# Attention in a five-stage convolution kernel: the receptance moved from a sigmoid and a gate into the column denominators

## The chip, the cores and the metric

The kernel runs on one core of a Trainium2 chip. Its engines are PE (matrix multiply), DVE (VectorE), ACT (ScalarE, which evaluates functions from a table that has to be loaded), POOL (GpSimd) and SP, which issues DMAs here. Each engine runs its own queue in order and waits on semaphores. The metric is the device time of one execution in microseconds, as the median of three runs.

## The reference

Two layers: a pointwise and a 13x13 depthwise convolution with GELU, then a block with attention and a feed-forward part, on 16 images of 192 channels and 56 x 56 pixels. What matters here is the attention:

```
k = xs2 @ att_wk.T
v = xs2 @ att_wv.T
sr = jax.nn.sigmoid(xs2 @ att_wr.T)
v = _wkv(sp_decay[0] / T, sp_first[0] / T, k, v)        # along rows
k2, v2 = k, v with rows and columns exchanged
v2 = _wkv(sp_decay[1] / T, sp_first[1] / T, k2, v2)     # along columns
v = v2 with rows and columns exchanged back
att_out = sr * v @ att_wo.T
tok = tok + gamma1 * att_out
```

`_wkv` is a recurrence over the 3136 pixels, channel by channel: a weighted running sum of v (numerator) over a running sum of weights (denominator), with a running maximum of the exponents to keep them in range. The last product is sr times the quotient of the column pass. With sr = 1 / (1 + exp(-r)), sr * N / D equals N / (D * (1 + exp(-r))).

## The kernel before

`build` runs six stages: `prepare`, `pointwise`, `depthwise` and `omni`, `attention`, a second `omni`, and `feed_forward`. Only `attention` (L820) is touched. It lies in the middle of the span.

**Tiles and steps.** The channels of two images make three tiles of 128 partitions; `TILES` is 24. A step s (0 to 24) does the row pass of tile s and the column pass of tile s-1. Each pass has 7 units of 448 pixels, so that a full step has 14 units, at positions 0 to 13; `ROWS_AT` = 3, 5, 6, 8, 9, 11, 12 are those by row, and 0, 1, 2, 4, 7, 10, 13 those by column. Step 0 has only rows, step 24 only columns.

**A unit.** DVE makes the running maximum O (`run_max`, a copy at L1259 or a memset at L1253, then the scan L1260), two units ahead. POOL subtracts it (`exponents`, L1203 and L1206). ACT exponentiates: L1109 gives the input factor E, L1114 the decay factor A. POOL multiplies E by v (`weigh`, L1216, into EV). DVE scans the sums Q and P (`sums`, L1265, both in PSUM), forms the denominator E = bonus * E + Q (L1281) and the numerator EV = bonus * EV + P (L1284), and keeps the last sums (L1286). ACT inverts the denominator as exp(-log(E)) (L1120, L1125). POOL multiplies numerator and inverse and writes the result over v (`divide`, L1223). For a column unit ACT first copies k column by column into E (`column_k`, L1134: source elements 224 bytes apart); for a row unit it evacuates k, v and r from PSUM (`evacuate`, L1100).

**The receptance.** r goes raw into `rS` (four slots). At position 11 of each step, `UNITS - 3`, ACT turns the whole tile into its sigmoid (`receptance`, L1104), which needs another function table than exp and log, and asks for the common table of both behind it (L1105). In step 0 nothing asks for the common table before that, and log and exp load their own by turns. At position 1 of step s DVE multiplies the finished tile s-2 by the sigmoid (`gate`, L1293, 3136 elements, both sources in SBUF). ACT's first evacuation of k in step s waits for that gate, since it overwrites the slots of tile s-2.

**The residual.** In steps 3, 4, 6, 7, ... 21, 22 and 24 an image finished by the step before is projected out on PE (`project_out`, L1054 and L1055, waits for the gate), added to the residual by DVE (`add_residual`, L1301, 7 groups at positions `RESIDUAL_AT` = 5, 7, 8, 10, 11, 12, 13) and squared by ACT (`squares`, L1140, four a group, in the unit behind; the last two groups, eight squares, come at the step's end). When the squares are done SP stores the image and loads the next residual input. The steps 2, 5, 8, ... 23 have no residual work.

**What sets the order.** Everything above is written by hand: the positions, and in each engine's loop the order of calls. In ACT's loop the unit two ahead comes first (`column_k` or the evacuations), then the exponentials of the next unit, then log and inverse of this one, then the squares.

## Time and profile before

| | us |
|---|---|
| median of 3 runs | 5882.12 (5879.2 to 5884.56) |
| the profiled execution, its own time | 5891.42 |
| its span | 5889.4 |
| PE busy | 4958.5 (84%) |
| ACT busy | 3768.7 (64%) |
| DVE busy | 3670.4 (62%) |
| POOL busy | 3455.7 (59%) |

The shares are means over all stages. In the profile's forty slices PE is above 90% in feed_forward, which fills the last third, while in the slices of attention, 11 to 24, DVE and ACT are the busiest. The chain of work that ended last goes back through feed_forward only and tells nothing of attention; that stage has to be read from its own windows and its own order of time.

### The profile page before, as it was taken

How to read it: one execution, taken by the hardware profiler on the slowest of the kernel's cores; microseconds unless marked ns; L12 is line 12 of the kernel's file. 1: busy time of each engine (PE TensorE's matmuls, PEld its weight loads, DVE VectorE, ACT ScalarE, POOL GpSimd, SP SyncE). 2: the span in 40 equal slices, each digit the busy share in tenths (PEclk: the TensorE clock that was granted, in tenths of full speed). 3: DMA queues.
4: the chain of work that ended last, by engine and by line, in shares of the span. 5: the costliest groups of instructions: out<-in, count | busy, mean ns of one | idle time of the engine just before them, and what ended most of it. 6: DMA issues, size and time to landing. Idle time of an engine off the chain costs nothing. (4 is left out here: it accounts for less than half of the span.)

```text
span 5889.4 us, 77955 instructions
## 1 busy us (share of the span) xinstructions
PE 4958.5 (84%) x23504; PEld 3925.9 (67%) x23504; DVE 3670.4 (62%) x5447; ACT 3768.7 (64%) x7142; POOL 3455.7 (59%) x2824
## 2 busy tenths in 40 slices
PE   5979999979866676767766663997999999999999
PEld 5969999967723343443434433776888888888888
DVE  4423333367669888898888885775555555555555
ACT  0017777656568888888888884665566556556655
POOL 0027777767658777687786773775444444444444
PEclk9989999989988888988888886998999999999999
DMA  6987777599820221223213123998322322322320
GB/s 169 265 206 192 191 189 198 136 237 261 223 68 23 77 55 45 66 55 78 58 42 83 30 65 93 250 262 214 72 57 68 74 57 63 80 55 63 82 55 24
DMA packets 388595, 674.48 MB, mean 115 GB/s; under 512 B 21117, under 2 KB 346702, under 8 KB 368910
## 3 DMA queue, kind: packets, MB, share of 16 engines
q1 hardware_dynamic: 334768, 514.71, 37.6%
q10 hardware_dynamic: 53522, 156.21, 7.1%
q8 instruction: 130, 2.13, 0.2%
q14 instruction: 175, 1.43, 0.1%
HBM read 437.00 MB, written 233.87 MB: 114 GB/s over the span
## 5 line engine op out<-in xcount | busy, mean ns | idle before, releaser
L1542 POOL TENSOR_TENSOR hidden_part<-hidden_whole,hidden_part 128x448 fp32r<-128x448 f32 x672 | 751.5, 1154 | 1027.2 <-ACT hidden_part L1507 1027.2
L676 POOL TENSOR_TENSOR omni_in_part<-omni_norm,omni_in_part 113x448 fp32r<-113x448 f32 x384 | 604.2, 1584 | 212.3 <-ACT omni_in_part L735 210.2
L1411 PE MATMUL f_out_ps<-hidden_part,ffn_wv_parts 128*128 128x448 f32 (+1 forms) x3360 | 721.8, 370 | 0.7 <-POOL hidden_part L1542 0.7
L1411 PEld LDWEIGHTS f_out_ps<-hidden_part,ffn_wv_parts 128*128 128x128 f32 (+1 forms) x3360 | 578.1, 177 | 104.6 <-POOL hidden_part L1542 35.3
L1216 POOL TENSOR_TENSOR input_times_v<-input_factor,v_all 128x448 f32<-128x448 f32 x336 | 419.6, 1249 | 362.6 <-ACT input_factor L1109 342.9
L1585 DVE TENSOR_SCALAR hidden_whole<-f_hid_ps 128x448 f32<-128x448 f32 x672 | 417.5, 622 | 250.7 <-POOL hidden_part L1542 157.4
L87 PE MATMUL omni_ps<-omni_in_part,omni_band_part 113*112 113x448 f32 x1152 | 439.0, 381 | 117.0 <-POOL omni_in_part L676 78.1
L1038 PE MATMUL proj_ps<-mixT_low,kvr_weights_low 128*128 128x448 f32 x672 | 353.9, 611 | 205.4 <-ACT k_all L1100 175.9
L1040 PE MATMUL proj_ps<-mixT_ends,kvr_weights_ends 128*128 128x448 f32 x1008 | 515.0, 594 | 0.0
L87 PE MATMUL dw_ps<-dw_in_part,dw_band_part 112*112 112x432 f32 (+3 forms) x1344 | 474.6, 353 | 41.9 <-POOL dw_in_part L477 41.9
L88 PE MATMUL dw_ps<-dw_in_part,dw_band_part 112*112 112x432 f32 (+3 forms) x1344 | 474.9, 353 | 0.0
L89 PE MATMUL dw_ps<-dw_in_part,dw_band_part 112*112 112x432 f32 (+3 forms) x1344 | 472.2, 351 | 0.0
L473 POOL TENSOR_TENSOR dw_band_part<-dw_band,dw_band_part 112x784 fp32r<-112x784 f32 x192 | 334.4, 1741 | 192.1 <-ACT dw_band_part L516 192.1
L88 PE MATMUL omni_ps<-omni_in_part,omni_band_part 113*112 113x448 f32 x1152 | 437.0, 379 | 0.0
L89 PE MATMUL omni_ps<-omni_in_part,omni_band_part 113*112 113x448 f32 x1152 | 436.8, 379 | 0.0
L1223 POOL TENSOR_TENSOR v_all<-input_times_v,input_factor 128x448 f32<-128x448 f32 x336 | 384.9, 1145 | 58.3 <-ACT input_factor L1125 58.3
L1054 PE MATMUL out_ps<-attention_out_weights,r_all 128*112 128x193 f32 x896 | 246.0, 359 | 200.6 <-DVE residual_pairs L1301 170.3
L516 ACT ACTIVATE dw_band_part<-dw_band 112x784 fp32r<-112x784 f32 x192 | 163.7, 853 | 390.1 <-DMA dw_band<-flat 383.1
L494 DVE TENSOR_TENSOR dw_sums<-dw_sums,dw_out 112x448 f32<-112x448 f32 x192 | 121.5, 633 | 456.4 <-ACT dw_out L545 456.4
L1507 ACT ACTIVATE hidden_part<-hidden_whole 128x448 fp32r<-128x448 f32 x672 | 389.0, 579 | 21.3
L1411 PE MATMUL f_hid_ps<-ffn_mixT_part,ffn_wk_high 128*128 128x448 f32 x1344 | 397.2, 377 | 5.3 <-DVE hidden_whole L1585 5.2
L1505 ACT ACTIVATE hidden_whole<-hidden_whole 128x448 f32<-128x448 f32 x672 | 379.2, 564 | 1.5 <-DVE hidden_whole L1585 0.8
(181 smaller groups left out, 13026.5 us busy)
## 6 DMA issues: line engine op xcount, KB each, us to landing
xin<-x SPq DMA_DIRECT2D x16, 2352.0 KB, 13.1
x_pointwise<-xp ACTq DMA_DIRECT2D x16, 2352.0 KB, 18.8
dw_in<-x_pointwise SPq DMA_DIRECT2D x24, 1568.0 KB, 24.4
y_gelu<-dw_out ACTq DMA_DIRECT2D x24, 1568.0 KB, 13.2
omni_in<-y_gelu SPq DMA_DIRECT2D x24, 1568.0 KB, 22.9
att_mix<-omni_out ACTq DMA_DIRECT2D x24, 1568.0 KB, 13.9
residual_pairs<-y_gelu SPq DMA_DIRECT2D x16, 2352.0 KB, 11.9
tok<-residual_pairs SPq DMA_DIRECT2D x16, 2352.0 KB, 9.0
```

The source lines that it names most:

```text
L87: pe.matmul(bank, w_hi, x_hi, start=start, stop=False)
L88: pe.matmul(bank, w_hi, x_lo, start=False, stop=False)
L89: return pe.matmul(bank, w_lo, x_hi, start=False, stop=stop)
L676: pool.tensor_tensor(rounded(inner(p[1])), z[u][:, :, cc, :], inner(p[0]), ALU.subtract).then_inc(in_split, 1)
L1040: pe.matmul(to[:, 0:TC], keep.w_end[:, o, part * 128:(part + 1) * 128], x_end[:, t, :], start=False, stop=True).then_inc(bank_ready, 1)
L1216: pool.tensor_tensor(grid(EV[unit.slot % 2]), grid(E[unit.slot]), part_of(vS, unit), ALU.mult).then_inc(ev_done, 1)
L1223: pool.tensor_tensor(part_of(vS, unit), grid(EV[unit.slot % 2]), grid(E[unit.slot]), ALU.mult).then_inc(wkv_done, 1)
L1411: return pe.matmul(bank, rounded(w), rounded(x), start=start, stop=stop)
L1505: act.activation(whole[h % KW][:, :], whole[h % KW][:, :], ACT.Square).then_inc(kk_ready, 1)
L1507: act.activation(rounded(kk[n % 2][0][:, h, :]), whole[h % KW][:, :], ACT.Copy).then_inc(kh_ready, 1)
L1542: pool.tensor_tensor(rounded(kk[n % 2][1][:, h, :]), whole[h % KW][:, :], kk[n % 2][0][:, h, :], ALU.subtract).then_inc(kl_ready, 1)
L1585: dve.tensor_scalar_max(whole[h % KW][:, :], hidden_bank(n, h)[:, 0:TC], 0.0).then_inc(relu_done, 1)
```

## The change

Receptance: r is evacuated through Exp with scale -1, so that `rS` holds exp(-r). The function `receptance` with its sigmoid, its table loads and its semaphore goes. `preload_act_table_set` for the common table of exp and log stands once, ahead of ACT's loop.

Column units: DVE makes the numerator and keeps the last sums first; then it writes bonus * E + Q over Q, in PSUM, and then (exp(-r) + 1) * Q into E, reading `rS` column by column. That makes three instructions and the copy behind the scans where there were two and the copy. Two of them wait for an instruction of DVE itself that stands right ahead (`kept`, `bonus_done`). Row units are as before. POOL's division of a column unit writes to `rS`, not to `vS`. The function `gate` goes; PE's output projection waits for the last division of the tile, and ACT's first evacuation of a step for the last product with v of tile s-2.

```diff
@@ evacuate, receptance @@
-                    need(act, g_done, step - 1)
+                    if step > 1:
+                        act.wait_ge(ev_done, unit_of[step - 2, False, NQ - 1].count())
...
-                act.activation(to[:, TC * t:TC * (t + 1)], bank(e)[:, 0:TC], ACT.Copy).then_inc(bank_read, 1)
-
-            def receptance(step):
-                act.wait_ge(bank_read, entry["project", step, NCH - 1, 2] + 1)
-                act.activation(rS[:, step % 4, :], rS[:, step % 4, :], ACT.Sigmoid).then_inc(sr_done, 1)
-                act.preload_act_table_set("natural_log_exp_and_others")
+                how = (ACT.Exp, -1.0) if o == 2 else (ACT.Copy, 1.0)
+                act.activation(to[:, TC * t:TC * (t + 1)], bank(e)[:, 0:TC], how[0], scale=how[1]
+                               ).then_inc(bank_read, 1)
...
+            act.preload_act_table_set("natural_log_exp_and_others")
             for step in range(TILES + 1):
...
-                    if rows and unit.position == UNITS - 3:
-                        receptance(step)
@@ project_out @@
-                    pe.wait_ge(g_done, 3 * pair + 2 + n)
+                    pe.wait_ge(wkv_done, unit_of[3 * pair + 1 + n, False, NQ - 1].count())
@@ divide @@
-                pool.tensor_tensor(part_of(vS, unit), grid(EV[unit.slot % 2]), grid(E[unit.slot]), ALU.mult
-                                   ).then_inc(wkv_done, 1)
+                to = part_of(vS, unit) if unit.rows else part_of(rS, unit)
+                pool.tensor_tensor(to, grid(EV[unit.slot % 2]), grid(E[unit.slot]), ALU.mult).then_inc(wkv_done, 1)
@@ outputs, gate @@
+            def numerator(unit):
+                ev = EV[unit.slot % 2][:, :]
+                dve.wait_ge(p_done, unit.count())
+                dve.scalar_tensor_tensor(ev, ev, unit.bonus, P, ALU.mult, ALU.add).then_inc(n_done, 1)
+
+            def keep_last(unit):
+                dve.tensor_copy(last[unit.slot][:, :], PQ[:, :, QT - 1]).then_inc(kept, 1)
+
             def outputs(unit):
-                e, ev = E[unit.slot][:, :], EV[unit.slot % 2][:, :]
+                e = E[unit.slot]
                 dve.wait_ge(q_done, unit.count())
-                dve.scalar_tensor_tensor(e, e, unit.bonus, Q, ALU.mult, ALU.add
-                                         ).then_inc(d_done, 1)
-                dve.wait_ge(p_done, unit.count())
-                dve.scalar_tensor_tensor(ev, ev, unit.bonus, P, ALU.mult, ALU.add
-                                         ).then_inc(n_done, 1)
-                dve.tensor_copy(last[unit.slot][:, :], PQ[:, :, QT - 1]).then_inc(kept, 1)
-
-            def gate(tile):
-                r = rS[:, tile % 4, :]
-                dve.wait_ge(sr_done, tile + 1)
-
-                dve.wait_ge(wkv_done, unit_of[tile, False, NQ - 1].count())
-                dve.tensor_tensor(r, vS[:, tile % 2, :], r, ALU.mult).then_inc(g_done, 1)
+                if unit.rows:
+                    dve.scalar_tensor_tensor(e[:, :], e[:, :], unit.bonus, Q, ALU.mult, ALU.add).then_inc(d_done, 1)
+                    numerator(unit)
+                    keep_last(unit)
+                    return
+
+                numerator(unit)
+                keep_last(unit)
+                dve.wait_ge(kept, unit.count())
+                dve.scalar_tensor_tensor(Q, e[:, :], unit.bonus, Q, ALU.mult, ALU.add).then_inc(bonus_done, 1)
+                dve.wait_ge(bonus_done, unit.tile * NQ + unit.q + 1)
+                dve.wait_ge(bank_read, entry["project", unit.tile, NCH - 1, 2] + 1)
+                dve.scalar_tensor_tensor(grid(e), part_of(rS, unit), 1.0, Q.rearrange("p (a b) -> p a b", b=W),
+                                         ALU.add, ALU.mult).then_inc(d_done, 1)
...
-                    if unit.position == 1 and step > 1:
-                        gate(step - 2)
...
-            gate(TILES - 1)
```

DVE's queue at position 1 of step 2, before (a scan is listed as SCALAR_TENSOR_TENSOR; `sums_state` holds Q and P; in brackets the semaphores that an instruction waits for):

```order
L1260 SCALAR_TENSOR_TENSOR run_max<-sums_state,run_max,input_factor 128x448
L1293 TENSOR_TENSOR r_all<-v_all,r_all 128x3136 [waits wkv_divided,receptance_ready]
L1265 SCALAR_TENSOR_TENSOR sums_state<-decay_factor,sums_last,input_factor 128x448 [waits sums_last_kept,denominator_done,decay_factor_ready,input_factor_ready]
L1265 SCALAR_TENSOR_TENSOR sums_state<-decay_factor,sums_last,input_times_v 128x448 [waits numerator_done,input_times_v_done]
L1281 SCALAR_TENSOR_TENSOR input_factor<-input_factor,wkv_bonus,sums_state 128x448 [waits denominator_scan_done]
L1284 SCALAR_TENSOR_TENSOR input_times_v<-input_times_v,wkv_bonus,sums_state 128x448 [waits numerator_scan_done]
L1286 COPY sums_last<-sums_state 128x2
L1253 MEMSET run_max 128x1 [waits projection_evacuated]
```

The same place now:

```order
L1257 SCALAR_TENSOR_TENSOR run_max<-sums_state,run_max,input_factor 128x448
L1262 SCALAR_TENSOR_TENSOR sums_state<-decay_factor,sums_last,input_factor 128x448 [waits sums_last_kept,denominator_done,decay_factor_ready,input_factor_ready]
L1262 SCALAR_TENSOR_TENSOR sums_state<-decay_factor,sums_last,input_times_v 128x448 [waits numerator_done,input_times_v_done]
L1278 SCALAR_TENSOR_TENSOR input_times_v<-input_times_v,wkv_bonus,sums_state 128x448 [waits numerator_scan_done,denominator_scan_done]
L1281 COPY sums_last<-sums_state 128x2
L1295 SCALAR_TENSOR_TENSOR sums_state<-input_factor,wkv_bonus,sums_state 128x448 [waits sums_last_kept]
L1298 SCALAR_TENSOR_TENSOR input_factor<-r_all,sums_state 128x448 [waits projection_evacuated,column_denominator_done]
L1250 MEMSET run_max 128x1 [waits projection_evacuated]
```

The gate between running maximum and first scan is gone; the denominator moved from ahead of the numerator to behind the copy, and became two instructions.

ACT's queue at positions 11 and 12 of step 1, before (L1120 and L1125 are log and inverse, L1134 the copy of k by column, for the unit two ahead):

```order
L1120 ACTIVATE input_factor<-input_factor 128x448
L1125 ACTIVATE input_factor<-input_factor 128x448
L1104 ACT_TABLE_LOAD
L1104 ACTIVATE r_all<-r_all 128x3136
L1105 ACT_TABLE_LOAD
L1134 ACTIVATE input_factor<-k_all 128x448
L1109 ACTIVATE input_factor<-input_factor 128x448
```

The same place now:

```order
L1118 ACTIVATE input_factor<-input_factor 128x448
L1123 ACTIVATE input_factor<-input_factor 128x448
L1132 ACTIVATE input_factor<-k_all 128x448
L1107 ACTIVATE input_factor<-input_factor 128x448
L1112 ACTIVATE decay_factor<-decay_exponent,wkv_decay 128x448
L1118 ACTIVATE input_factor<-input_factor 128x448
```

The two loads and the sigmoid between inverse and copy are gone. In the whole stage ACT's queue had 59 table loads, and has one.

## Rows read from the trace of the kernel before

**Rows 1.** Busy time by windows: a step without residual work, and one with it.

```profile
core 0: us, PE busy (x) PEld busy (x) DVE busy (x) ACT busy (x) POOL busy (x), PEclk, DMA share, GB/s
2262.99:2331.48 68.49, 38.91 (x92) 18.68 (x92) 65.80 (x101) 53.95 (x92) 62.01 (x57) 0.75 0.26 66
2331.48:2418.14 86.66, 66.05 (x249) 44.46 (x250) 73.11 (x115) 73.70 (x156) 62.08 (x57) 0.87 0.18 43
```

**Rows 2.** Timeline, a residual step's end: start, length, engine, line, tiles, idle before.

```profile
2392.82 1.28 ACT L1104 ACT_TABLE_LOAD   x1
2394.11 2.82 ACT L1104 ACTIVATE r_all<-r_all 128x3136 f32<-128x3136 f32 x1
...
2402.03 1.09 DVE L1260 TENSOR_TENSOR_SCAN run_max<-sums_state,input_factor 128x448 f32<-128x448 f32 x1 [5.34 <-issue]
...
2417.01 0.15 DVE L1259 COPY run_max<-run_max 128x1 f32<-128x1 f32 x1 [3.84 <-ACT input_factor L1134]
...
2418.14 4.08 DVE L1293 TENSOR_TENSOR r_all<-v_all,r_all 128x3136 f32<-128x3136 f32 x1
...
2418.90 4.16 POOL L1203 TENSOR_TENSOR input_factor<-input_factor,run_max 128x448 f32<-128x448 f32 x1
...
2422.14 1.15 DVE L1265 TENSOR_TENSOR_SCAN sums_state<-decay_factor,sums_last,input_factor 128x448 f32<-128x448 f32 x1
```

**Rows 3.** Groups by line, whole stage: count, busy us, mean ns, idle before.

```profile
L1125 ACT ACTIVATE input_factor<-input_factor 128x448 f32<-128x448 f32 x336 | 193.9, 577 | 8.2
L1120 ACT ACTIVATE input_factor<-input_factor 128x448 f32<-128x448 f32 x336 | 191.2, 569 | 2.1 <-DVE input_factor L1281 2.0
L1134 ACT ACTIVATE input_factor<-k_all 128x448 f32<-128x448 f32 x168 | 174.6, 1039 | 0.1
...
L1301 DVE TENSOR_TENSOR residual_pairs<-out_ps,residual_pairs 112x386 f32<-112x386 f32 x218 | 109.6, 542 | 34.6 <-DMA residual_pairs<-y_sums 24.6 <-PE out_ps L1055 10.1
L1293 DVE TENSOR_TENSOR r_all<-v_all,r_all 128x3136 f32<-128x3136 f32 x24 | 97.5, 4062 | 0.0
...
L1104 ACT ACTIVATE r_all<-r_all 128x3136 f32<-128x3136 f32 x24 | 67.6, 2817 | 0.3
...
L1104 ACT ACT_TABLE_LOAD x24 | 30.8, 1283 | 0.4
...
L1120 ACT ACT_TABLE_LOAD x5 | 6.4, 1283 | 0.1
```

**Rows 4.** Timeline, DVE, the stage's end: the last gate, the last image's first residual.

```profile
3580.38 3.41 DVE L1293 TENSOR_TENSOR r_all<-v_all,r_all 128x3136 f32<-128x3136 f32 x1
...
3608.37 1.03 DVE L1301 TENSOR_TENSOR residual_pairs<-out_ps,residual_pairs 112x386 f32<-112x386 f32 x2 [24.57 <-DMA residual_pairs<-y_sums]
```

**Rows 5.** Timeline, DVE, behind the sigmoids of step 0 and of step 8.

```profile
1699.37 1.09 DVE L1260 TENSOR_TENSOR_SCAN run_max<-sums_state,input_factor 128x448 f32<-128x448 f32 x1 [7.74 <-issue]
...
2321.66 1.09 DVE L1260 TENSOR_TENSOR_SCAN run_max<-sums_state,input_factor 128x448 f32<-128x448 f32 x1 [2.69 <-issue]
```

**Rows 6.** Timeline, DVE, one unit in step 8 from its second scan on.

```profile
2281.14 1.12 DVE L1265 TENSOR_TENSOR_SCAN sums_state<-decay_factor,sums_last,input_times_v 128x448 f32<-128x448 f32 x1
2282.18 0.65 DVE L1281 SCALAR_TENSOR_TENSOR input_factor<-input_factor,wkv_bonus,sums_state 128x448 f32<-128x448 f32 x1
2282.75 0.67 DVE L1284 SCALAR_TENSOR_TENSOR input_times_v<-input_times_v,wkv_bonus,sums_state 128x448 f32<-128x448 f32 x1
2283.34 0.14 DVE L1286 COPY sums_last<-sums_state 128x2 f32<-128x2 f32 x1
2283.41 0.13 DVE L1259 COPY run_max<-run_max 128x1 f32<-128x1 f32 x1
```

**Rows 7.** Timeline, DVE in `prepare`, where each instruction waits for the one ahead.

```profile
23.05 0.76 DVE L225 TENSOR_TENSOR sc<-bcv,sd 128x576 f32<-128x576 f32 x1
23.84 0.76 DVE L226 TENSOR_TENSOR sh<-bcv,sc 128x576 f32<-128x576 f32 x1
```

**Rows 8.** One line, POOL's product with v: shortest, median and longest ns.

```profile
L1216 POOL TENSOR_TENSOR input_times_v<-input_factor,v_all x336: 1127/1249/1395, 1650.9 to 3571.7; 128x448 f32<-128x448 f32 x168
```

More of the change, by code:

```diff
@@ L852, in attention @@
         kt_done = m.sem("k_by_column_done")
-        sr_done = m.sem("receptance_ready")
-        g_done = m.sem("wkv_gated")
+        bonus_done = m.sem("column_denominator_done")
         out_ps_ready = m.sem("attention_out_in_psum")
@@ L960, in part_of @@
         def part_of(t, unit):
+            slot = unit.tile % t.shape[1]
             if unit.rows:
-                return t[:, unit.tile % 2, unit.q * QT:(unit.q + 1) * QT].rearrange("p (a b) -> p a b", b=W)
-            by_column = t[:, unit.tile % 2, :].rearrange("p (r w) -> p w r", r=W)
+                return t[:, slot, unit.q * QT:(unit.q + 1) * QT].rearrange("p (a b) -> p a b", b=W)
+            by_column = t[:, slot, :].rearrange("p (r w) -> p w r", r=W)
             return by_column[:, unit.q * QW:(unit.q + 1) * QW, :]
```

## The prediction, made before the changed kernel was run

> **What bounds the kernel now.** The change touches one stage, attention, in the middle of the span; the chain that ended last covers only feed_forward, so I read the stage by its windows first. What the reader is to see in them is how much of each step DVE is busy. A step is 14 units of work (7 by row, 7 by column). A step without residual work (8 of the 24) takes 68.49 us with DVE busy 65.80; a step with it (14) takes 86.66 us with DVE at 73.11 and ACT at 73.70 [rows 1]. So DVE sets the pace in the first kind, and in the second DVE and ACT take turns: the timeline of a step's end shows DVE idle for 5.34 and 3.84 us, both times for ACT's L1134, the copy of k by column, which stands in ACT's queue behind the sigmoid with its two table loads, and behind eight squares [rows 2]. Between such stalls a unit costs DVE 4.4 us back to back. POOL's unit is nearly as long, but its growth is nil here.
>
> **What goes.** (a) The gate, L1293, 24 times, 4062 ns in the mean [rows 3]. It stands in DVE's queue between a running maximum and a scan: 2418.14 to 2422.14 is 4.0 us on the path [rows 2]. POOL's subtraction beside it takes 4.16 us, so POOL is held too. 23 gates lie inside the steps. The 24th is hidden already: the last image then waits for its residual input, which lands at 3608.37 [rows 4].
> (b) The sigmoid: 2817 ns and two loads of 1283 ns [rows 3], 5.4 us of ACT per step. In a step with residual work ACT is behind, so all of it counts. In a step without, DVE idles 2.69 us for it [rows 5], and only that comes back.
> (c) In step 0 ten loads, five before L1120 [rows 3] and as many before L1125, because nothing asks for the common table before the first sigmoid, and one before L1109. Each stands on ACT's chain of evacuations. 11 x 1.28 = 14 us, and 5.4 for step 0's sigmoid, behind which DVE idles 7.74 us [rows 5]: 19.5. PE may come next in this step, so I take 17 (12 to 19.5).
> The loads themselves: at 2392.82 a load of 1.28 us begins and the sigmoid follows 1.29 us later [rows 2]. The Trainium skill, "ScalarE: Activation LUTs", section "What ACT_TABLE_LOAD costs", adds a DRAIN of about 1380 ns to every switch. By that page the 48 loads of sigmoid and preload would be worth 66 us more, as an estimate; this trace disagrees, since no such gap stands between load and next instruction.
>
> **What comes.** The receptance as exp(-r) rides on its evacuation, an activation of the same shape; it costs nothing new. The sigmoid's work reappears on DVE in every column unit, 168 times. Before, from the second scan: start of P 2281.14, L1281 2282.18, L1284 2282.75, L1286 2283.34, next unit's L1259 2283.41: 2.27 us [rows 6]. After: P must be finished before the numerator: 1.12 plus 0.03 for a DVE wait on DVE (0.76 us of work, next start after 0.79 [rows 7]) is 1.15; numerator to copy 0.59; copy 0.15 + 0.03, since the first new instruction overwrites Q; that one 0.65 + 0.03; the second x - 0.07, which overlaps the next. Sum 2.53 + x.
> x, the length of the second new instruction, is the one unknown: it reads rS down the columns, 224 bytes from element to element, and no DVE row does that. Bounds: 0.65 (as L1281, if the stride is free; L1301 reads 386 elements, two neighbours each 112 bytes, in 542 ns, full rate [rows 3]); 0.88 (POOL's L1216 takes 1127 ns at least and 1249 in the middle, half its 336 units being by column; a column one so takes about 1370, some 0.23 more [rows 8]); 1.11 (ACT's L1134 reads kS with this stride in 1039 ns where L1125, dense, takes 577 [rows 3]: 0.46 more); 1.3 (ACT's own ratio: from 448 to 3136 dense elements ACT goes from 577 to 2817 ns [rows 3], so 0.833 ns for one and 204 ns of start; the stride makes 373 ns of elements into 835, 2.24 times. The gate without POOL beside it, 3.41 us for 3136 [rows 4], gives DVE 1.03 ns for one, 0.46 of L1281's 0.65; 0.19 + 2.24 x 0.46 is 1.22, and 1.3 with a margin). I take 1.11: ACT's is the plainest analogue, one pass over the same pattern. Then a column unit costs DVE 3.64 instead of 2.27, +1.37; with 0.65, +0.91; with 1.3, +1.56.
> The Trainium skill speaks to this stride twice. "SBUF — State Buffer", section "Door 1: The DMA port swizzle", says that lines are 16 bytes and that full bandwidth wants at least two hits per line; L1301 has two, L1134 one, and the trace agrees for both. "VectorE: DVE Perf Modes", section "Mode 1× (REGULAR)", says the plain mode takes fp32 and "weird strides" as they come; that would be x = 0.65, the first rival below.
>
> **Who pays.** Fully: step 1, 7 units; the 8 steps without residual work, 6 each, 48; the position-0 units of step 2 and of the 7 residual steps that follow one without, 8; positions 1 and 2 of 14 residual steps, 28; step 24, which has seven columns and where ACT's backlog of squares takes up part, 5. That is 96. Partly: positions 4 and 7 of the 14 residual steps, where DVE has short idles already: 0.6 us a step, 8. Not at all: positions 10, 13 and the following 0 of these steps. I followed one end: without the sigmoid ACT's L1134 frees DVE's running maximum 5.4 us earlier, at 2396.6 instead of 2402.03, and DVE, which was ready 5.34 us before that, at 2396.7, doesn't idle; three longer units then fill most of the 3.84 us before the next L1134, and the logarithm waits a little for the later denominator. The next first scan comes 8.9 us earlier, of 9.4 (4.0 + 5.4). Behind the new waits in DVE's queue stands the next running maximum, for which POOL waits; it moves with the unit and is in the 1.37.
>
> **Sum.** Gains: 14 x 8.9 = 125; 9 ends of other steps x (4.03 + 2.69) = 60; step 0, 17; together 202. Costs: 96 x 1.37 = 132, and 8; together 140. Net -62. The profiled execution took 5891.42 us (span 5889.4) and would take 5829; the median of the runs shown is 5882.12, 9.3 less, so 5820. With x = 1.3 the costs grow by 96 x 0.19 + 3 = 21: 5841. PE, POOL and the other stages keep their times. PE no longer waits for the gate, but waits mostly for ACT and residuals anyway.
>
> **Rivals.** *The stride is free* (x = 0.65): costs 96 x 0.91 + 3 = 90, gains 4 more, net -116: 5766. For: DVE is the slower reader, one element in 1.04 ns. Against: L1134 [rows 3]. In between, x = 0.88, lies 5792.
> *Nothing is absorbed, slower.* In a column unit the denominator is ready some 2.0 us later after P than now. ACT's queue holds log, inverse, up to eight squares and then L1134 behind it. If ACT arrives at the log before the denominator at positions 4, 7, 10, 13 and 0, its squares and the next L1134 slip by what DVE lost, and the idle time absorbs nothing: 5 x 14 x 1.37 = 96, of which I counted 8 and 7: +81 on 5820, 5901. It decides if ACT waits at L1120 by more than about 1 us in each. Against: at L1120 ACT waited for DVE only 2.0 us in the whole stage [rows 3], and in residual steps it comes 1 to 3 us late by itself. The same sign, but only with both, comes from x near 1.7.
> *ACT was not held*: if PE's evacuations, not the loads, pace ACT's tail, the sigmoid's 5.4 us give 2.69 as elsewhere: 14 x 2.7 = 38 less gained, 5858. Against: ACT is dense over that tail.
> *The table isn't kept*: if Exp and Ln still ask for tables by turns, hundreds of loads come. The order of instructions shows one load in the stage where 59 stood; excluded.
>
> **How the numbers follow.** Forecast with x from 1.0 to 1.3: chance 0.5, 5805 to 5841, point 5820. Stride free or nearly (x under 1.0): 0.28, 5766 to 5805. ACT not held: 0.12, 5840 to 5865, a little of which falls within 0.2% (11.8 us) of 5882. Nothing absorbed: 0.06. Others, either side: 0.04. About 0.2% is what a measurement of this kernel can tell from no change. The range is 5755 to 5862: from the free stride's time with 11 us below it, to the case where ACT was not held; what lies outside is the slower rival, the upper end of that case and the others, less than 2 in 10. Faster 0.88, within 0.2% 0.06, slower 0.06.
>
> **What would show it.** In the profile after: the second new instruction's mean tells x; one table load in the stage; steps without residual work at about 71.5 us (before 68.5), with it at about 81 (before 86.7); step 0 some 17 us shorter; DVE's idle before the running maximum at position 0 gone from 5.34 and 2.69. I am wrong if ACT's wait at the log grows to tens of us, if residual steps stay above 85, or if the numerator or the new PSUM write is longer than 0.7 us.

## The result, and the profile after

| | before | after |
|---|---|---|
| median of 4 runs each, us | 5880.66 (5878.55 to 5884.56) | 5826.92 (5820.87 to 5830.1) |
| profiled execution, us (its span) | 5891.42 (5889.4) | 5820.87 (5819.0) |
| ratio of the times | | 0.991, 95% interval 0.989 to 0.992 |

The change took 54 us off (0.9%). The forecast was 5820 and the range 5755 to 5862. Four more runs had a median of 5822.56 against 5883.15, 61 us less. The two profiled executions are 70.4 us apart in span, but not all of that is the change: from the first row unit of the stage to the last image's first residual they differ by 59.4 us. The other 11 us lie ahead of and behind this stretch, in code that is the same in both. Over the profiled executions of all kernels here that part takes 3907 to 3920 us, so a single span can mislead by up to 13 us. Two of all the runs below were slow ones, 8545 us of b_table_once and 18638 us of a_k_on_pool; the ratios leave them out, and each moves its kernel's median by 1 us at most.

The windows of the kernel after, to be held against [rows 1]. The first is a step without residual work, the others are two with it; columns as there.

```profile
core 0: us, PE busy (x) PEld busy (x) DVE busy (x) ACT busy (x) POOL busy (x), PEclk, DMA share, GB/s
2234.85:2306.14 71.29, 41.00 (x96) 20.07 (x95) 70.07 (x107) 48.91 (x86) 58.00 (x56) 0.77 0.18 43
2306.14:2386.81 80.67, 64.51 (x256) 42.09 (x255) 76.94 (x121) 69.92 (x155) 59.94 (x57) 0.92 0.26 65
2386.81:2469.63 82.82, 65.95 (x255) 35.30 (x254) 77.53 (x122) 65.73 (x145) 58.87 (x57) 0.89 0.30 77
```

A step without residual work grew from 68.5 to 71.3 us and is now filled by DVE (70.1 busy). One with it fell from 86.7 to 81.8 in the mean of 14, with DVE busy 77 and ACT 66 to 70. So the kernel loses in one kind and gains in the other.

The groups by line that answer to [rows 3]. L1298 is the second new instruction, L1295 the first, L1118 the logarithm (L1120 before).

```profile
L1298 DVE SCALAR_TENSOR_TENSOR input_factor<-r_all,sums_state 128x448 f32<-128x448 f32 x168 | 167.0, 994 | 5.7
...
L1295 DVE SCALAR_TENSOR_TENSOR sums_state<-input_factor,wkv_bonus,sums_state 128x448 f32<-128x448 f32 x168 | 115.8, 689 | 6.0
...
L1118 ACT ACTIVATE input_factor<-input_factor 128x448 f32<-128x448 f32 x336 | 192.1, 572 | 83.6 <-DVE input_factor L1298 81.3 <-DVE input_factor L1287 1.7
...
L1132 ACT ACTIVATE input_factor<-k_all 128x448 f32<-128x448 f32 x168 | 174.5, 1039 | 0.0
...
L1102 ACT ACTIVATE r_all<-proj_ps 128x448 f32<-128x448 f32 x168 | 91.1, 542 | 95.0 <-PE proj_ps L1040 94.2
...
L1141 ACT ACT_TABLE_LOAD x1 | 1.3, 1283 | 7.4 <-PEq L571 7.4
```

x, the one unknown of the forecast, is 994 ns. One load of a table stands in the stage. The evacuation that now makes exp(-r) takes 542 ns, like those of k and v (535 and 536). And ACT's wait for DVE at the logarithm has grown from 2.0 to 81.3 us, which the forecast named as a sign that it is wrong; the experiments have to explain that.

The end of a residual step on the timeline, where [rows 2] showed DVE idle for 5.34 and 3.84 us:

```profile
2214.33 1.09 DVE L1257 TENSOR_TENSOR_SCAN run_max<-sums_state,input_factor 128x448 f32<-128x448 f32 x1 [0.32 <-issue]
...
2227.95 1.01 ACT L1132 ACTIVATE input_factor<-k_all 128x448 f32<-128x448 f32 x1
...
2228.99 0.15 DVE L1256 COPY run_max<-run_max 128x1 f32<-128x1 f32 x1 [1.31 <-ACT input_factor L1132]
```

One column unit from its second scan on, which answers to [rows 6]:

```profile
2231.16 1.13 DVE L1262 TENSOR_TENSOR_SCAN sums_state<-decay_factor,sums_last,input_times_v 128x448 f32<-128x448 f32 x1
2232.40 0.68 DVE L1278 SCALAR_TENSOR_TENSOR input_times_v<-input_times_v,wkv_bonus,sums_state 128x448 f32<-128x448 f32 x1
2232.99 0.15 DVE L1281 COPY sums_last<-sums_state 128x2 f32<-128x2 f32 x1
2233.18 0.69 DVE L1295 SCALAR_TENSOR_TENSOR sums_state<-input_factor,wkv_bonus,sums_state 128x448 f32<-128x448 f32 x1
2233.91 1.00 DVE L1298 SCALAR_TENSOR_TENSOR input_factor<-r_all,sums_state 128x448 f32<-128x448 f32 x1
2234.84 1.08 DVE L1257 TENSOR_TENSOR_SCAN run_max<-sums_state,k_all 128x448 f32<-128x448 f32 x1
```

From scan to next unit 3.68 us; the forecast had 3.64, and 2.27 before. The stage's end, to [rows 4]: the last image's residual still comes late, now after 26.82 us of idle instead of 24.57.

```profile
3545.22 1.03 DVE L1307 TENSOR_TENSOR residual_pairs<-out_ps,residual_pairs 112x386 f32<-112x386 f32 x2 [26.82 <-DMA residual_pairs<-y_sums]
```

### The profile page after: what moved, and what is told of

Same layout as the page of the kernel before. It is cut to its first block and busy times, and to the rows that moved or that the text cites. A ratio compares the mean times of both kernels' runs of the same rounds, so it can differ in the third digit from the quotient of the medians.

```text
span 5819.0 us, 78329 instructions
## 1 busy us (share of the span) xinstructions
PE 4976.5 (86%) x23504; PEld 3933.2 (68%) x23504; DVE 3770.2 (65%) x5591; ACT 3640.0 (63%) x7060; POOL 3380.8 (58%) x2824
## 5 line engine op out<-in xcount | busy, mean ns | idle before, releaser
L1040 PE MATMUL proj_ps<-mixT_ends,kvr_weights_ends 128*128 128x448 f32 x1008 | 528.7, 609 | 0.0
L1040 PEld LDWEIGHTS proj_ps<-mixT_ends,kvr_weights_ends 128*128 128x128 f32 x1008 | 196.9, 209 | 281.5 <-issue 281.5
L1038 PEld LDWEIGHTS proj_ps<-mixT_low,kvr_weights_low 128*128 128x128 f32 x672 | 137.0, 216 | 359.9 <-ACT k_all L1102 218.1
```

The source lines that it names most:

```text
L1038: pe.matmul(to[:, 0:TC], keep.w_low[:, o, 0:LOW], low[kind // 2], start=True, stop=False)
L1040: pe.matmul(to[:, 0:TC], keep.w_end[:, o, part * 128:(part + 1) * 128], x_end[:, t, :], start=False, stop=True).then_inc(bank_ready, 1)
```

## A table by step, for all kernels

DVE clears one element of `run_max` when a tile's first unit by row begins. From these marks on the timeline each step can be cut out (step 0 from its own mark to that of step 1; the end of the stage from the mark of step 23 to the last image's first residual). "Without" are 7 of the steps without residual work (2, 5, ... 20), "with" the 14 residual steps, both means. "Against before" is a kernel's median minus that of the kernel before, run beside it on the same chip (5880.7 to 5885.4); kernels that weren't run side by side are compared by this column.

| kernel | step 0 | without | with | end | median | against before |
|---|---|---|---|---|---|---|
| before | 75.7 | 68.5 | 86.8 | 126.9 | 5883 | |
| after | 58.2 | 71.3 | 81.8 | 136.4 | 5826.9, 5822.6 | -54, -61 |
| b_table_once | 60.9 | 68.6 | 86.8 | 127.3 | 5868.5 | -15 |
| b_no_gate | 75.5 | 65.7 | 85.0 | 122.6 | 5830.0 | -54 |
| b_no_sigmoid | 55.5 | 65.2 | 81.3 | 123.8 | 5754.2 | -129 |
| b_neither | 55.4 | 62.4 | 79.7 | 119.3 | 5703.0 | -181 |
| b_columns_changed | 78.1 | 77.4 | 91.0 | 142.7 | 6024.8 | +139 |
| a_dense_r | 58.2 | 69.3 | 79.8 | 132.1 | 5782.5 | -101 |
| a_short_squares | 58.2 | 71.3 | 78.8 | 132.5 | 5776.2 | -109 |
| a_k_on_pool | 59.4 | 72.3 | 79.7 | 137.5 | 5811.9 | -71 |
| a_r_by_column | 57.5 | 69.1 | 80.0 | 131.9 | 5778.9 | -104 |
| a_both | 57.5 | 69.1 | 78.7 | 132.1 | 5758.0 | -127 |
| r_sum_in_sbuf | 57.2 | 66.2 | 79.5 | 127.3 | 5740.7 | -145 |

## The experiments

My theory is the sum on record: gains of 202 us and costs of 140. Its rival is that both are smaller and happen to differ by as much. The first four kernels take the gains apart, starting from the kernel before.

**The table alone.**

```diff
+            act.preload_act_table_set("natural_log_exp_and_others")
             for step in range(TILES + 1):
                 done = finished(step)
```

> The kernel before with one edit: the table of both functions is asked for once ahead of ACT's loop; the sigmoid with its two loads and the gate stay. Full output. My account: only step 0 gains. Ten loads by turns and the one at the first exponential, 11 x 1.28 = 14 us, stand on ACT's chain of evacuations there, so 10 to 14 us less than before, 5867 to 5871. Rival: PE or DVE paces step 0, and the loads lie beside it: 0 to 4 us.

Measured: ratio 0.997 (0.996 to 0.998), 15 us less, all of it in step 0 (75.7 to 60.9). The loads stood on the path of that step and nothing hid them. The account was right, and its 14 us too.

**The gate alone.**

```diff
-                    if unit.position == 1 and step > 1:
-                        gate(step - 2)
...
-                pool.tensor_tensor(part_of(vS, unit), grid(EV[unit.slot % 2]), grid(E[unit.slot]), ALU.mult
-                                   ).then_inc(wkv_done, 1)
+                to = part_of(vS, unit) if unit.rows else part_of(rS, unit)
+                pool.tensor_tensor(to, grid(EV[unit.slot % 2]), grid(E[unit.slot]), ALU.mult).then_inc(wkv_done, 1)
```

> The kernel before without the product of the receptance and the weighted mean (left out: the 24 gates; POOL writes the column results to the place the output projection reads; sigmoid and loads stay). My account: 23 gates on the path at 4.03 us, 93 us less: 5788. Rival, ACT paces the steps with residual work, so that the gate is only hidden idle time there: 9 gates at 4.03, 36 to 45 us less, about 5840.

Measured: ratio 0.991 (0.990 to 0.993), 54 us less. That lies between the two, and both were wrong. A step without residual work gives back 2.8 of the gate's 4.0 us, a residual one 1.9. On DVE's timeline of this kernel an idle stretch has appeared where the gate stood, before the running maximum that waits for the first evacuation of k:

```profile
2313.92 1.09 DVE L1261 TENSOR_TENSOR_SCAN run_max<-sums_state,k_all 128x448 f32<-128x448 f32 x1 [1.19 <-issue]
```

The gate had covered 1.2 us of another wait there. A further wait stands right behind it, at the first scan of the residual step that begins here:

```profile
2313.03 1.70 PE L1038 MATMUL proj_ps<-mixT_low,kvr_weights_low 128*128 128x448 f32 x2
...
2315.97 0.54 ACT L1101 ACTIVATE v_all<-proj_ps 128x448 f32<-128x448 f32 x1 [1.63 <-PE proj_ps L1040]
2316.41 0.63 ACT L1115 ACTIVATE decay_factor<-decay_exponent,wkv_decay 128x448 f32<-128x448 f32 x1
...
2317.13 1.16 DVE L1266 TENSOR_TENSOR_SCAN sums_state<-decay_factor,sums_last,input_factor 128x448 f32<-128x448 f32 x1 [2.12 <-ACT decay_factor L1115]
```

```profile
core 0: us, PE busy (x) PEld busy (x) DVE busy (x) ACT busy (x) POOL busy (x), PEclk, DMA share, GB/s
2304.00:2310.00 6.00, 1.88 (x9) 1.53 (x9) 6.00 (x10) 5.62 (x11) 5.84 (x6) 0.50 0.00 1
2310.00:2316.00 6.00, 6.00 (x9) 2.91 (x10) 3.82 (x7) 1.30 (x4) 4.60 (x6) 0.54 0.00 0
2316.00:2322.00 6.00, 5.64 (x20) 2.99 (x18) 4.62 (x8) 5.57 (x11) 3.42 (x4) 1.00 0.01 3
```

The scan waits for ACT's decay factor, which stands in ACT's queue behind the evacuation of v, and that waits for PE. The projections run at the lower level of PE's clock here: PE had been idle for 15.84 us up to 2305.53 and, behind eight short products, for 2.59 us more; the granted clock from 2304 to 2310 us is 0.50 (1.2 GHz) and a pair of these products takes 1.70 us; from 2316 us on it is 1.00 (2.4 GHz) and a pair takes 0.91. In the kernel before, these projections run beside the gate. In the 14 residual steps DVE now waits 1.2 us in the mean within 4 us of the step's mark, where it waited for nothing before.

**The sigmoid and its loads alone.**

```diff
-                    if rows and unit.position == UNITS - 3:
-                        receptance(step)
...
-                dve.wait_ge(sr_done, tile + 1)
+                dve.wait_ge(bank_read, entry["project", tile, NCH - 1, 2] + 1)
...
+            act.preload_act_table_set("natural_log_exp_and_others")
```

> The kernel before without the sigmoid and its two loads per step and with the table asked for once (left out: the sigmoid; the gate multiplies the raw receptance). My account: 5.4 us in each of 14 residual steps (less 0.5 that is given back), 2.69 in 9 others, 17 in step 0: 110 us less, 5771. Rival (ACT was not held): 2.7 in all 23 and 17: 79 us less, 5802.

Measured: ratio 0.979 (0.977 to 0.980), 129 us less, more than expected. Residual steps give 5.6 us (the sigmoid and two loads last 5.4), the others 3.3 (2.69 expected), step 0 gives 20 us (17). "ACT was not held", which gave 79 us, is out: ACT's work counts fully in residual steps.

**Both.** The two edits above together.

> The kernel before with neither gate nor sigmoid and with the table asked for once; the column units stay as they were (left out: the receptance's part in the output). This is the gains' side of my sum by itself: 202 us less, 5679; what the changed kernel is above it is the costs' side, 140 by my sum and 148 if I misjudged nothing but the sum. Rival (the extra column work is absorbed more than I said, and the gains are smaller): 150 to 180 less, and so a cost side of 95 to 125.

Measured: ratio 0.969 (0.968 to 0.971), 181 us less. The two single gains add up (54 + 129 = 183). So the gains' side is 181, not 202, and the changed kernel, 54 to 61 below the kernel before, stands 120 to 127 above this one, not 140. A residual step of this kernel:

```profile
2261.89:2341.72 79.83, 64.22 (x251) 42.14 (x250) 69.21 (x113) 69.00 (x153) 58.43 (x56) 0.91 0.24 60
```

DVE and ACT are both busy 69 of 80 us: neither fills the step, and they still wait for each other in turn. The wait for L1134's copy behind eight squares, 3.84 in [rows 2], is still 3.40 in it:

```profile
2195.02 0.15 DVE L1254 COPY run_max<-run_max 128x1 f32<-128x1 f32 x1 [3.40 <-ACT input_factor L1130]
```

**The costs alone.** The column units of the changed kernel in the kernel before:

```diff
+                numerator(unit)
+                keep_last(unit)
+                dve.wait_ge(kept, unit.count())
+                dve.scalar_tensor_tensor(Q, e[:, :], unit.bonus, Q, ALU.mult, ALU.add).then_inc(bonus_done, 1)
+                dve.wait_ge(bonus_done, unit.tile * NQ + unit.q + 1)
+                dve.wait_ge(sr_done, unit.tile + 1)
+                dve.scalar_tensor_tensor(grid(e), part_of(rS, unit), 1.0, Q.rearrange("p (a b) -> p a b", b=W),
+                                         ALU.add, ALU.mult).then_inc(d_done, 1)
```

> The kernel before, with gate, sigmoid and its loads, and with the column units of the changed kernel added (changed: the column denominators are multiplied by 1 plus the sigmoid as well). The costs' side of my sum without the gains. If DVE pays for all but positions 4, 7, 10, 13 and 0, as predicted, 120 to 140 more than before, about 6015. If ACT's slowness covers the extra work in the residual steps wholly (they stay at 86.9) and only steps without it grow, 68.5 to 75: 65 to 90 more, about 5960.

Measured: ratio 1.024 (1.022 to 1.025), 139 us more, the first of the two. Steps without residual work take 8.9 more, residual ones 4.1. The same units cost 8.9 and 2.1 where gate and sigmoid are gone (after against b_neither, 71.3 - 62.4 and 81.8 - 79.7). So costs and gains aren't independent. Without the stall behind the sigmoid (5.6 us), DVE is idle for 8.2 us of a residual step in the kernel before and for 10.4 in b_neither. The longer column units fill 4.1 us of the first and 5.7 of the second: 4.1 and 4.7 are left. And in a step without residual work the sigmoid's stall doesn't absorb them: it is 2.63 us in b_columns_changed, against 2.69 before. ACT starts the sigmoid only behind a logarithm that now waits for DVE, so the stall moves along.

**The stride.** In the changed kernel, L1298 with dense reading:

```diff
-                dve.scalar_tensor_tensor(grid(e), part_of(rS, unit), 1.0, Q.rearrange("p (a b) -> p a b", b=W),
-                                         ALU.add, ALU.mult).then_inc(d_done, 1)
+                r, how = part_of(rS, unit), ALU.add
+                if unit.tile > 1:
+                    r, how = grid(rS[:, (unit.tile + 2) % 4, unit.q * QT:(unit.q + 1) * QT]), ALU.max
+                dve.scalar_tensor_tensor(grid(e), r, 1.0, Q.rearrange("p (a b) -> p a b", b=W),
+                                         how, ALU.mult).then_inc(d_done, 1)
```

> The changed kernel with the second new DVE instruction reading 448 dense elements of rS instead of elements 224 bytes apart, for all tiles but the first two (left out: the true receptance; it reads another tile's slot and takes the larger of it and 1 instead of 1 plus it). Theory, the stride alone makes it long: mean 0.65 to 0.69 us instead of 0.994, so 0.3 less in each column unit where DVE sets the pace (8 steps without residual work and step 24, 7 units each, 19 us) and 0 to 4 in the 14 others: 19 to 23 less than the changed kernel. By the weights of my prediction (96 units) 29. Rival, the length comes from reading SBUF and PSUM together and not from the stride: 0.

 

> The changed kernel, unedited, beside the kernels that are held against it. Full output. Expected 5827, ratio 0.990 to 0.992.

Measured: 5782.5, ratio to before 0.983 (0.982 to 0.984), where the changed kernel beside it has 0.990 (0.988 to 0.991): 40 us less. The mean over the stage, in which the first two tiles are still read with the stride:

```profile
L1301 DVE SCALAR_TENSOR_TENSOR input_factor<-r_all,sums_state 128x448 f32<-128x448 f32 x168 | 109.4, 651 | 5.7
```

Those 14 units take 0.99 us each, as before; the 154 others take 0.62. So the stride alone makes it long, by 0.37 us of 0.994. But 40 us are more than the 19 to 23 that I expected, or the 29 by the weights of the forecast. Residual steps fell by 1.8 to 2.0 us, nearly as much as the others (2.0 to 2.2): after this edit they stand at 79.8, where b_neither, without any of the new work, has 79.7. So the first 1.0 us that a column unit adds is covered there, and of the last 0.37 (2.6 us in seven units) three quarters or more are paid.

**exp(-r) by column.** The same, with the true result:

```diff
+                to, take = to[:, TC * t:TC * (t + 1)], bank(e)[:, 0:TC]
+                if o == 2:
+                    h = TC // W
+                    to = rS[:, step % 2, :].rearrange("p (w r) -> p w r", r=W)[:, :, h * t:h * (t + 1)]
+                    take = take.rearrange("p (r w) -> p w r", w=W)
+                act.activation(to, take, how[0], scale=how[1]).then_inc(bank_read, 1)
...
-                dve.scalar_tensor_tensor(grid(e), part_of(rS, unit), 1.0,
+                dve.scalar_tensor_tensor(grid(e), grid(rS[:, unit.tile % 2, unit.q * QT:(unit.q + 1) * QT]), 1.0,
```

> The changed kernel with exp(-r) written by ACT in column order (w outer, runs of 8 elements, from PSUM elements 224 bytes apart), rS with two slots, the final result in vS with four, so that the second new DVE instruction reads dense. Full output. Theory: DVE gains as with dense reading (19 to 23 less than the changed kernel) if ACT's evacuation keeps its 0.58 us. Rival: a PSUM source with 224-byte stride costs ACT the 0.46 that an SBUF source with it does: 7 x 0.46 = 3.2 us more per step on ACT, which paces the residual steps: 14 x 3.2 = 45 more, less 19, so some 20 to 25 above the changed kernel.

Measured: 5778.9, ratio to before 0.982 (0.981 to 0.983), 44 us below the changed kernel. The rival is out: ACT reads PSUM with the stride of 224 bytes and writes runs of eight elements at no cost (542 ns in the changed kernel and here), and DVE's L1301 takes 620.

```profile
L1301 DVE SCALAR_TENSOR_TENSOR input_factor<-r_by_column,sums_state 128x448 f32<-128x448 f32 x168 | 104.2, 620 | 5.7
L1107 ACT ACTIVATE r_by_column<-proj_ps 128x448 f32<-128x448 f32 x168 | 91.1, 542 | 90.3 <-PE proj_ps L1040 90.3
```

**Who paces a residual step of the changed kernel?** Two kernels take work off ACT. The first shortens its squares:

```diff
-                    act.activation(junk[:, :], Y[:, 0:C, j], ACT.Square, accum_out=s2[:, j:j + 1]
+                    act.activation(junk[:, 0:8], Y[:, 0:8, j], ACT.Square, scale=20.0, accum_out=s2[:, j:j + 1]
```

> The changed kernel with ACT's squares of the residual taken over 8 of 192 channels (left out: the other 184 in the sum; the count of instructions and waits stays). Some 0.3 us less of ACT for each of 56 squares of a residual step, 17 us. Theory, ACT paces the residual steps: they fall from 81.8 to the 77 that DVE is busy, about 14 x 4.5 and some 10 at the end of the stage, 60 to 80 less than the changed kernel's 5823; steps without residual work stay at 71.3. Rival, the extra column work on DVE paces them already: 79 or more stay, 20 to 30 less.

Measured: 5776.2, ratio to before 0.982 (0.980 to 0.984), 109 us less than before where the changed kernel has 54 to 61: some 50 for ACT's relief, between the two. The square's mean fell from 560 to 214 ns, 19 us of ACT per residual step, and the step fell by 3.0:

```profile
2295.63:2374.51 78.88, 65.53 (x261) 42.39 (x259) 76.74 (x122) 61.19 (x156) 60.48 (x57) 0.94 0.27 70
```

With 19 us of ACT gone, 2 us of DVE's idle time are left. So ACT is one limit, and DVE is the next, 3 us below it.

The second gives the copy of k by column to POOL:

```diff
             for unit in line:
                 before, after = near(unit, -1), near(unit, 1)
+                column_k(near(unit, 2))
...
+                pool.tensor_copy(grid(E[unit.slot]), part_of(kS, unit)).then_inc(kt_done, 1)
```

> The changed kernel with the copy of k by column (7 per step, 1.04 us each on ACT) made by POOL ahead of its product, so that DVE's running maximum no longer stands behind ACT's squares. Full output. Theory, ACT paces the 14 residual steps (81.8 us, DVE busy 77): they fall to 77 to 79, 40 to 60 less than the changed kernel; steps without residual work stay. Rival: POOL with 7 more copies (about 1.25 us each, 66 of 71 us busy in a step without residual work) becomes the one that the others wait for: those steps grow by 2 to 5, residual steps gain nothing, +15 to +50.

Measured: 5811.9, ratio to before 0.988 (0.986 to 0.990), 11 us below the changed kernel. Residual steps fell to 79.7 (77 to 79 expected), and the others grew by 1.0, as the rival said in kind: POOL is busy for 65.6 us of such a step instead of 57.9, and DVE waits 0.9 us in it for POOL's product, for which it didn't wait before. Of the theory the direction held, of the size half. One more thing stands in this kernel's groups: ACT waits longer at the logarithm than in the changed kernel (126.6 us instead of 83.6), and the kernel is faster.

```profile
L1119 ACT ACTIVATE input_factor<-input_factor 128x448 f32<-128x448 f32 x336 | 192.2, 572 | 126.6 <-DVE input_factor L1299 113.3 <-DVE input_factor L1288 12.0
```

**Faster versions.** a_both takes exp(-r) by column and lets POOL make only those copies of k that are issued in a residual step:

```diff
+        def by_pool(unit):
+            return finished(line[unit.n - 2].step) is not None
```

> exp(-r) kept by column, and the copy of k by column made by POOL where it is issued in a step with residual work, by ACT in the others. Full output. Steps without residual work stay at 69.1; residual steps, 79.8 with either edit alone, fall to 77 to 78, since each edit relieves another engine: 20 to 40 less than with exp(-r) by column alone, 5740 to 5760. Rival: a third limit (PE and ACT's evacuations) holds residual steps at 79.4 to 80: no gain, 5775 to 5780.

Measured: 5758.0, ratio to before 0.979 (0.977 to 0.980), 127 us less than before where a_r_by_column has 104: 23 us, at the weak end of what was expected. Residual steps reach 78.7, not 77 to 78.

r_sum_in_sbuf also has exp(-r) by column, and orders the column unit otherwise:

```diff
-                numerator(unit)
-                keep_last(unit)
-                dve.wait_ge(kept, unit.count())
-                dve.scalar_tensor_tensor(Q, e[:, :], unit.bonus, Q, ALU.mult, ALU.add).then_inc(bonus_done, 1)
+                dve.scalar_tensor_tensor(e[:, :], e[:, :], unit.bonus, Q, ALU.mult, ALU.add).then_inc(bonus_done, 1)
+                numerator(unit)
+                keep_last(unit)
...
-                dve.scalar_tensor_tensor(grid(e), grid(rS[:, unit.tile % 2, unit.q * QT:(unit.q + 1) * QT]), 1.0,
-                                         Q.rearrange("p (a b) -> p a b", b=W), ALU.add, ALU.mult)
+                dve.scalar_tensor_tensor(e[:, :], rS[:, unit.tile % 2, unit.q * QT:(unit.q + 1) * QT], 1.0, e[:, :],
+                                         ALU.add, ALU.mult)
```

> exp(-r) kept by column, with the first new instruction writing E in SBUF straight behind the scans (no wait for the copy of the last column), then numerator, copy, and the second with both sources in SBUF. Full output. Two waits of DVE on itself go: 0.1 to 0.2 less per column unit, 7 x 9 units, 6 to 12 less than 5779. Rival: two sources in SBUF hold POOL up, as the gate does (its subtraction 0.98 to 4.16 us beside it): DVE's instruction 0.65 to 0.8 and POOL's operations in the mean 0.1 longer, 0 to 15 more.

Measured: 5740.7, ratio to before 0.976 (0.974 to 0.977), 145 us less than before, 41 more than a_r_by_column and the fastest of all, where 6 to 12 were expected. A column unit on DVE's timeline:

```profile
1856.80 1.14 DVE L1265 TENSOR_TENSOR_SCAN sums_state<-decay_factor,sums_last,input_times_v 128x448 f32<-128x448 f32 x1
1857.85 0.66 DVE L1295 SCALAR_TENSOR_TENSOR input_factor<-input_factor,wkv_bonus,sums_state 128x448 f32<-128x448 f32 x1
1858.42 0.68 DVE L1281 SCALAR_TENSOR_TENSOR input_times_v<-input_times_v,wkv_bonus,sums_state 128x448 f32<-128x448 f32 x1
1859.01 0.16 DVE L1284 COPY sums_last<-sums_state 128x2 f32<-128x2 f32 x1
1859.08 0.62 DVE L1300 SCALAR_TENSOR_TENSOR input_factor<-r_by_column,input_factor 128x448 f32<-128x448 f32 x1
```

Scan to next instruction is 1.05 us instead of the 1.24 of the changed kernel above, copy to next 0.07 instead of 0.19, and the 0.15 between the two new instructions (0.73 for a 0.69 us instruction against 0.57 to 0.59 here) is gone too: 0.46 us a unit, 3.2 in seven, of which the step without residual work gave back 2.8. In the profiled executions the stage is 34 us shorter than a_r_by_column's, so of the 41 some 7 aren't explained by it. I had counted only the gap behind an instruction's end, and forgotten that without a wait the next one starts some 0.08 us before that end. The rival showed itself, but small: POOL's product takes 1350 ns in the mean instead of 1248, and L1300 673 instead of 620. It is the overlap that does it: the 89 products that run beside L1300 for more than 0.3 us take 1.61 us in the mean, the 240 that don't touch it 1.26. In a_r_by_column, where the second new instruction has one source in PSUM, those beside it take 1.22 and the others 1.26.

```profile
L1217 POOL TENSOR_TENSOR input_times_v<-input_factor,v_all 128x448 f32<-128x448 f32 x336 | 453.4, 1350 | 261.2 <-ACT input_factor L1111 241.1 <-POOL v_all L1224 1.3 <-ACT r_by_column L1107 0.4
```

a_both and r_sum_in_sbuf weren't tried together.

## Why the prediction was right, and where it wasn't

The time was right to 7 us because two terms were too large, the gains by 21 us and the costs by 13 to 20, and stood on opposite sides. That they came out nearly equal was luck.

**x.** Taken as 1.11, measured 0.994, inside the bounds; halfway between POOL's 0.88 and ACT's 1.11. The stride costs DVE 0.37 us (a_dense_r), where ACT's copy takes 0.46 more than a dense one. "The stride is free" is out. The unit as a whole came out at 3.68 us against 3.64: the wait behind the scan was 0.09 longer than I had it, the one between the new instructions 0.05, and x with what it overlaps 0.11 shorter. The sentence of the Trainium skill on lines of 16 bytes ("SBUF — State Buffer", section "Door 1: The DMA port swizzle") is borne out by this trace for DVE as well: 0.994 us with one element per line, 0.620 dense. The one on "weird strides" ("VectorE: DVE Perf Modes", section "Mode 1× (REGULAR)") says that the plain mode works with them. That they cost nothing, as the forecast read it for x = 0.65, isn't borne out.

**Step 0.** Forecast 17 us shorter; 17.5 measured. Its gain alone is 20.3 (b_neither), slightly over the upper bound of 19.5: the loads gave their 14.8 in full and the sigmoid the rest, nothing else came next. Two longer column units take 2.7 of it back.

**Ends of steps without residual work.** Forecast 6.72 us for gate and sigmoid; 6.1 measured (68.5 to 62.4). The sigmoid was worth 3.3 instead of 2.69, the gate 2.8 instead of 4.03. Over nine ends 58 against 60.

**Ends of residual steps.** This is the step that failed: "The next first scan comes 8.9 us earlier, of 9.4". Measured 7.2 (86.8 to 79.7), 14 times, so 100 us and not 125. The sigmoid's 5.4 were there (5.6 measured), the gate's 4.03 were not: 1.9 alone, 1.6 when the sigmoid is out. I had followed one end of a step, up to the next first scan, and had not asked what else that scan waits for. More than half of the missing time stands right there: once the gate is gone, DVE waits at this scan for ACT's decay factor, behind PE's projections at the lower clock, 1.2 us a residual step in b_no_gate and 1.5 in b_neither, of the 2.2 and 2.4 that are missing. The forecast had no term for PE; it said that PE keeps its time. The wait behind the eight squares is as long as before (3.6 us in the kernel before and in the three without gate, sigmoid or both). This is read in the traces; no run changes PE's projections alone. What an instruction costs on the path at one place was taken for what the step gains.

**Costs.** 140 forecast. By themselves, in the kernel before, they are 139, with 8.9 in a step without residual work, where the forecast's weights give 7 x 1.37 = 9.6 from mark to mark, and 4.1 in a residual one, where they give two units and 0.6, 3.3. The weights described the kernel before well. In the kernel without gate and sigmoid the same units cost 120 to 127, because a residual step then pays 2.1. The forecast added two terms each of which had been read in the kernel before, and in the residual steps the second is smaller once the first is taken: this is what made up for the gains that were missing.

**The signs announced.** One table load, steps of about 71.5 (71.3) and 81 (81.8), step 0 17 us shorter and the idle time before the running maximum gone (0.32 instead of 5.34) all came. The sign for "wrong", ACT's wait at the log in the tens of us, came too, and was a bad sign. It adds up waits over the stage, and most are in steps that DVE fills, where ACT has nothing better to do: 7.1 us in the first window above, with ACT busy 48.9 of 71.3. The first row is from there, the others are from the residual step next to it:

```profile
ACT input_factor L1118 <- DVE input_factor L1298: 7.1, 5, 2.0
...
DVE run_max L1256 <- ACT input_factor L1132: 1.7, 1, 1.7
...
ACT input_factor L1118 <- DVE input_factor L1287: 0.2, 1, 0.2
ACT input_factor L1118 <- DVE input_factor L1298: 0.2, 1, 0.2
```

These are the waits of one window each (us in total, times, longest). The rival's own condition, more than 1 us at each of five positions of a residual step, didn't hold: ACT waits there for L1298 0.6 us a step in the mean of the 14. And a_k_on_pool, faster with a still longer wait, shows that the total by itself tells nothing.

**The end of the stage** grew by 9.5 us; the forecast's weights give 7.0 for it (five units of step 23 and five of step 24 at 1.37, less 2.69 and 4.03). Against b_neither it grew by 17.1, 1.4 for each of its twelve column units: all pay there, ACT's backlog covers none.

What stays open: why the residual steps of b_neither, a_dense_r, a_r_by_column and r_sum_in_sbuf all stop at 79.5 to 80 us although DVE is busy only 69 to 74.5 in them. ACT's queue is one reason, since with shorter squares a step of 78.8 has DVE busy 76.7. It isn't the only one: a_both, with ACT busy 62 and DVE 74, still takes 78.7. The wait at a step's first scan, behind PE's projections, is a part: 0.5 to 1.5 us a residual step in these kernels, 1.3 of the 4.4 us for which DVE is idle in a_both. No run separates what makes up the rest (POOL, PE, or the chain from one engine to the next and back within a unit).

## What to carry to other kernels

Where two engines take turns at the pace, a gain or a loss read at one place of the loop isn't yet that of the loop: the gate's 4.0 us gave back 1.9, the sigmoid's 2.69 gave 3.3. Ask what else the next instruction waits for. And measure gains and costs each by a kernel of its own before adding them, since here 202 and 140 forecast were 181 and 120 to 127 measured, and only the difference was right. Name a sign of failure for the stretch in which it would hurt, not for the whole stage: a wait of an engine that has nothing else to do is free. And when work is moved to the engine that sets the pace, look at its layout and at its waits on itself first; here these two were worth some 35 to 45 us each, together more than the change.

## What the runs showed of the hardware

- DVE, 448 fp32 elements of SBUF read 224 bytes apart, with a PSUM operand: 994 ns, against 620 dense. ACT has 1039 against 577 for the same pattern, POOL's plain copy with it 1016 (a_k_on_pool).
- ACT reading PSUM 224 bytes apart and writing SBUF in runs of 32 bytes: 542 ns, the same as dense.
- A wait of DVE on its own last instruction costs 0.12 to 0.2 us from start to start, not the 0.03 that stands behind the end: 1.24 against 1.05 behind a scan, 0.19 against 0.07 behind a small copy.
- Two SBUF operands on DVE slow POOL's own work down: its subtraction beside the gate took 4.16 us [rows 2] and takes 0.978 in the mean where the gate is gone; beside a 448-element instruction with two SBUF operands POOL's product takes 1.61 us where it takes 1.26 alone (r_sum_in_sbuf), and with one operand in PSUM it isn't stretched (1.22, a_r_by_column).
- PE's projections of 448 columns at the start of a step, behind 15.84 us of idle PE, take 1.70 us a pair at a granted clock of 0.50 (1.2 GHz) and 0.91 at 1.00 (2.4 GHz; b_no_gate).
